# A decoder layer on one core: first cross-attention operands loaded in the interleaved pass, distance rows in the first phase

## What is computed

```python
x = x + attention(layernorm(x))                     # self-attention, 224 keys
x = x + cross_attention(layernorm(x), ctx)          # 750 keys, with a distance bias
x = x + mixture(layernorm(x))                       # 8 experts, the best 2 of each token
# cross-attention:
rel = abs(arange(Nk)[None, :] - arange(Nq)[:, None] - (Nk - Nq))
scores = einsum('bhqd,bhkd->bhqk', q, k) / sqrt(32) - slopes[:, None, None] * rel
attn = softmax(scores)
```

## Time and profile before

| | |
|---|---|
| median of 3 runs | 1952.62 us (1949.11 to 1953.68) |
| the profiled execution | 1952.63 us, span 1951.0 us |
| mean granted TensorE clock | 0.956 |
| TensorE / weight loads | 1771.3 us (91%) / 1423.1 us (73%) |
| VectorE | 1089.2 us (56%) |
| ScalarE | 761.1 us (39%) |
| GpSimd | 563.7 us (29%) |
| DMA | mean 160 GB/s |

### The profile page before, as it was taken

The page is one execution under the profiler, slowest core; times in us unless marked ns, Lnnn a source line. Parts: engine busy times, 40 slices in busy tenths (PEclk is TensorE's granted clock), DMA queues, the critical chain, the costliest instruction groups (busy, mean ns, idle before and its releaser), DMA issues. The chain is left out here.

```text
span 1951.0 us, 35771 instructions
## 1 busy us (share of the span) xinstructions
PE 1771.3 (91%) x11824; PEld 1423.1 (73%) x11824; DVE 1089.2 (56%) x1865; ACT 761.1 (39%) x1376; POOL 563.7 (29%) x597
## 2 busy tenths in 40 slices
PE   6997999999998866999999999649999999999997
PEld 5886777777777754777777777438787787887776
DVE  5543555555555524767777677374554545446553
ACT  3223334444434323655455554232442424224432
POOL 0001111111111102444454454251433425215541
PEclk9997999999999986999999999759999999999999
DMA  7636665565656349967576671153674637355753
GB/s 236 201 137 167 179 172 156 157 195 158 190 174 172 97 117 175 178 148 158 124 161 146 145 156 47 49 186 122 210 237 113 210 108 225 104 172 185 265 167 86
DMA packets 210770, 311.41 MB, mean 160 GB/s; under 512 B 20520, under 2 KB 149992, under 8 KB 206008
## 3 DMA queue, kind: packets, MB, share of 16 engines
q1 hardware_dynamic: 186208, 222.24, 42.9%
q0 software_dynamic: 14288, 41.26, 9.5%
q10 hardware_dynamic: 10160, 46.38, 6.5%
HBM read 226.07 MB, written 83.74 MB: 159 GB/s over the span
## 5 line engine op out<-in xcount | busy, mean ns | idle before, releaser
L1725 DVE TENSOR_REDUCE a_part_max<-a_s_bank 112x1 f32<-112x500 f32 (+1 forms) x384 | 238.0, 673 | 108.4 <-PE a_s_bank L1500 77.8
L1640 ACT ACTIVATE a_prob<-a_st_bank 125x448 f32<-125x448 f32 x384 | 195.0, 545 | 125.3 <-PE a_st_bank L1518 88.3
L2321 DVE TENSOR_TENSOR e_u_sb<-e_u_bank,e_b_row 128x512 f32<-128x512 f32 x138 | 95.0, 689 | 244.5 <-PE e_u_bank L2076 244.5
L2074 PE MATMUL e_u_bank<-e_w_hi,e_xT_hi 128*128 128x512 f32 x552 | 221.6, 401 | 2.6 <-DVE e_xT_lo L2309 1.9
L2076 PE MATMUL e_u_bank<-e_w_hi,e_xT_lo 128*128 128x512 f32 x552 | 217.4, 394 | 0.0
L2075 PE MATMUL e_u_bank<-e_w_lo,e_xT_hi 128*128 128x512 f32 x552 | 216.4, 392 | 0.0
L1423 POOL TENSOR_TENSOR a_part_sum<-a_prob 125x448 f32<-125x448 f32 x128 | 146.6, 1145 | 184.0 <-ACT a_prob L1640 184.0
L1500 PE MATMUL a_s_bank<-a_k_st,a_q_st 104*112 104x500 f32 (+1 forms) x512 | 159.9, 356 | 37.4 <-DMA a_k_st<-k 23.3
L2144 ACT ACTIVATE e_g_hi<-e_g_bank 128x256 fp32r<-128x256 f32 x137 | 52.6, 384 | 331.7 <-PE e_g_bank L2083 321.7
L1518 PEld LDWEIGHTS a_st_bank<-a_q_st,a_k_st 104*125 104x125 f32 x768 | 146.8, 198 | 45.1 <-ACT a_prob L1640 16.0
L1518 PE MATMUL a_st_bank<-a_q_st,a_k_st 104*125 104x224 f32 x768 | 155.9, 287 | 15.3 <-ACT a_prob L1640 13.3
(11 more groups left out here) (300 smaller groups left out, 4152.9 us busy)
## 6 DMA issues: line engine op xcount, KB each, us to landing
e_w_raw<-L_ffn_Wl SPq DMA_DIRECT2D x96, 512.0 KB, 10.0
a_k_st<-k SPq DMA_DIRECT2D x96, 375.0 KB, 6.0
e_b_row<-L_ffn_bl ACTq DMA_DIRECT2D x35, 1024.0 KB, 5.8
k<-m_kt_hi SPq DMA_DIRECT2D x48, 250.0 KB, 2.9
k<-m_kt_lo SPq DMA_DIRECT2D x48, 250.0 KB, 3.7
m_c_in<-ctx POOLq DMA_DIRECT2D x12, 896.0 KB
m_q_st<-q SPq DMA_DIRECT2D x96, 112.0 KB, 3.1
m_k_st<-k SPq DMA_DIRECT2D x96, 112.0 KB, 3.0
```

What stands on the lines that cost most here:

```text
L1640: act.activation(prob[:, s % 2, hh, 2 * u:2 * u + 2, :], st_bank[n % SB][0:CR, 0:2 * S].rearrange("p (e q) -> p e q", e=2), ACT.Exp).then_ ...
L1725: dve.tensor_reduce(out, scores, AX.X, ALU.max).then_inc(s_free, 1)
L2074: pe.matmul(out, xT_hi[:, slot, k, :], w_h, start=(k == 0), stop=False)
```

## The change

Three parts.

The operands of cross step 0, with their distance rows, get a tensor of their own, `first` (16 KB in a partition), which outlives the interleaved pass. It lies where the raw weights of the first phase lay; these get two slots in place of three, so that each weight is loaded behind the one it replaces. In step 28 of the interleaved pass SyncE loads `first` with eight DMAs (`load_first`).

The distance rows are made in the first phase. GpSimd makes the ramps and the key rows and stores the latter, all after it has issued the loads of chunks 1 and 2. The 16 query slopes are tied to the 16 query and key blocks of chunks 1 and 2 (`head_beside`): two operations on ScalarE, one on VectorE, a store from GpSimd's queue for each head; `q_rows` has one buffer.

In the cross-attention SyncE loads, for steps 1, 2 and 3 in turn, distance rows, queries and keys, and the values of the step before; then the router's biases and weights; then operands of step 4, values 3, `w_raw` and `out_bias`. `small_loaded` counts three transfers. x1 of the first sequence is loaded and gets its bias in steps 2 and 3, and the output weights are split in step 3 in place of 2.

```diff
-    raw_at = {"wq": 0, "wk": 1, "wv": 2, "wo": 0, "m_wk": 1, "m_wv": 2, "m_wq": 0}
+    raw_at = {"wq": 0, "wk": 1, "wv": 0, "wo": 1, "m_wk": 0, "m_wv": 1, "m_wq": 0}
...
+        grid = c.sb("z_grid", [R8, S])
+        is_lo = c.sb("z_is_lo", [R8, 1])
+        k_lin = c.sb("z_k_lin", [R8, CTX])
+        q_lin = c.sb("z_q_lin", [R8, S])
+        q_lin_hi = c.sb("z_q_lin_hi", [R8, S], F32R)
+        q_rows = c.sb("z_q_rows", [R8, S], F32R)
...
+        def head_beside(n, ch, m):
+
+            at = ring_of(n, ch, m) - 2 * KT
+            return at if 0 <= at < HEADS else None
...
                 load_w("wk")
-                load_w("wv")
                 sp.dma_start(v_bias[:, :], biases["wv"].partition_broadcast(P)).then_inc(bias_loaded, DMA)
-                load_w_behind("wo", "wq")
+                load_w_behind("wv", "wq")
                 for ch in range(CHUNKS):
                     for m in range(KT):
                         store_t("wq", ch, m)
                     if ch == 0:
-                        load_w_behind("m_wk", "wk")
+                        load_w_behind("wo", "wk")
                     if ch == 1:
-                        load_w_behind("m_wq", "wo")
+                        load_w_behind("m_wv", "wo")
                     for m in range(KT):
                         store_t("wk", ch, m)
                     if ch == 0:
-                        load_w_behind("m_wv", "wv")
+                        load_w_behind("m_wk", "wv")
+                    if ch == 1:
+                        sp.wait_ge(w_ready["m_wk"], KT)
+                        sp.sem_inc(turn, 1)
+                        load_w("m_wq")
...
+                load_x(1)
+                load_x(2)
...
+                for hh in range(4):
+                    for fill in (1.0, 0.0):
+                        then(pool.affine_select(out=k_lin[0:4, :], in_=k_lin[0:4, :], compare_op=ALU.not_equal, fill=fill, base=-hh,
+                                                pattern=[[0, CTX]], channel_multiplier=1))
+                        if fill:
+                            pool.dma_start(k_rows_out[:, hh, :], k_lin[:, :]).then_inc(krows_stored, DMA)
+                            pool.wait_ge(krows_stored, (hh + 1) * DMA)
+                load_x(3)
...
+                for hd in range(HEADS):
+                    pool.wait_ge(qrows_ready, hd + 1)
+                    pool.sem_inc(turn, 1)
+                    pool.dma_start(q_rows_out[:, hd // 4, hd % 4, :], as_f32(q_rows[:, :])).then_inc(qrows_stored, DMA)
+                pool.wait_ge(qrows_stored, HEADS * DMA)
...
+                    if head_beside(n, ch, m) is not None:
+                        query_slopes(head_beside(n, ch, m))
+
+                def query_slopes(hd):
+                    act.wait_ge(grid_ready, 1)
+                    if hd:
+                        act.wait_ge(qrows_ready, hd)
+                    act.activation(q_lin[:, :], grid[:, :], ACT.Copy, scale=slope(hd))
+                    act.activation(q_lin_hi[:, :], grid[:, :], ACT.Copy, scale=slope(hd)).then_inc(qlin_ready, 1)
...
+                    hd = head_beside(n, ch, m)
+                    if hd is not None:
+                        dve.wait_ge(qlin_ready, hd + 1)
+                        if hd:
+                            dve.wait_ge(qrows_stored, hd * DMA)
+                        dve.scalar_tensor_tensor(q_rows[:, :], as_f32(q_lin_hi[:, :]), is_lo[:, :], q_lin[:, :], ALU.mult, ALU.add).then_inc(qrows_ready, 1)
...
+def first_parts(first):
+
+    rows = 3 * DH + 8
+    return (first[0:rows, 0:4 * S].rearrange("p (h t) -> p h t", h=4),
+            first[0:rows, 4 * S:4 * (S + CTX)].rearrange("p (h t) -> p h t", h=4))
...
+                def load_first():
+
+                    first_q, first_k = first_parts(first)
+                    for i in range(RING):
+                        sp.wait_ge(k_stored[i], RING * 2 * DMA)
+                    for m in range(KT):
+                        sp.wait_ge(q_stored[m], 2 * DMA)
                     sp.sem_inc(turn, 1)
...
+                    for r, (q_part, k_part) in enumerate(zip(QUERY_PARTS, KEY_PARTS)):
+                        rows = slice(DH * r, DH * r + DH)
+                        for tile, dram, part, n in ((first_q, q2, q_part, S), (first_k, k2, k_part, CTX)):
+                            sp.dma_start(as_f32(tile[rows, :, :]), dram[0, part, :, 0:n].rearrange("(h p) t -> p h t", p=DH)).then_inc(first_loaded, DMA)
+                    sp.dma_start(as_f32(first_k[KA:KA + 8, :, :]), k_rows).then_inc(first_loaded, DMA)
+                    sp.dma_start(as_f32(first_q[KA:KA + 8, :, :]), q_rows[:, 0, :, :]).then_inc(first_loaded, DMA)
...
-                    if s in (7, 8, 9, 10):
-                        store_key_rows(s - 7)
-                    if s in (12, 14, 16, 18):
-                        store_query_rows((s - 12) // 2)
+                    if s == STEPS - 4:
+                        load_first()
...
+        first_q, first_k = first_parts(first)
+        q_st = [first_q] + [c.sb(f"a_q_st{i}", [KB, 4, S], F32R) for i in range(1, SLOTS)]
+        k_st = [first_k] + [c.sb(f"a_k_st{i}", [KB, 4, CTX], F32R) for i in range(1, SLOTS)]
...
-                load_qk(0)
-                load_qk(1)
-                load_v(0)
-                sp.dma_start(w_raw[:, :, :], w_out.rearrange("(k p) n -> p k n", p=P)).then_inc(w_loaded, DMA)
-                sp.dma_start(out_bias[:, :], b_out.partition_broadcast(P)).then_inc(small_loaded, DMA)
+                def load_rows(i):
+                    sp.dma_start(as_f32(k_st[i][KQ:KB, :, :]), k_rows).then_inc(rows_loaded[i], DMA)
+                    sp.dma_start(as_f32(q_st[i][KQ:KB, :, :]), q_rows[:, i, :, :]).then_inc(rows_loaded[i], DMA)
+
+                for i in range(1, SLOTS):
+                    load_rows(i)
+                    load_qk(i)
+                    load_v(i - 1)
                 sp.dma_start(r_bias[:, :], b_route.partition_broadcast(QR)).then_inc(small_loaded, DMA)
                 sp.dma_start(c_bias[:, :], choice_bias.partition_broadcast(QR)).then_inc(small_loaded, DMA)
                 sp.dma_start(wr_raw[:, :], w_route).then_inc(small_loaded, DMA)
-                load_qk(2)
-                load_v(1)
-                load_qk(3)
-                load_v(2)
-                load_v(3)
+                load_qk(SLOTS)
+                load_v(SLOTS - 1)
+                sp.dma_start(w_raw[:, :, :], w_out.rearrange("(k p) n -> p k n", p=P)).then_inc(w_loaded, DMA)
+                sp.dma_start(out_bias[:, :], b_out.partition_broadcast(P)).then_inc(bias_loaded, DMA)
                 for s in range(STEPS):
-                    if s + SLOTS < STEPS:
+                    if s + SLOTS < STEPS and s:
                         load_qk(s + SLOTS)
-                        if s:
-                            load_v(s + SLOTS - 1)
+                        load_v(s + SLOTS - 1)
                     elif s + SLOTS == STEPS:
                         load_v(STEPS - 1)
...
                 pool.sem_inc(rel_ready, 1)
-                load_x(0)
                 then(pool.memset(ones[:, :], 1.0))
                 then(pool.iota(iota_e[:, :, :], pattern=[[0, 4], [1, EXPERTS]], base=0, channel_multiplier=0, allow_small_or_imprecise_dtypes=True))
                 then(pool.memset(before[:, 0, :], 0.0))
                 pool.sem_inc(const_ready, 1)
-                pool.wait_ge(small_loaded, 4 * DMA)
-                add_out_bias(0)
...
+                    if s == 2:
+                        load_x(0)
+                    if s == 3:
+                        pool.wait_ge(bias_loaded, DMA)
+                        add_out_bias(0)
...
-                diagonal_rests(0)
                 for hh in range(4):
                     maxima(0, hh)
-                    if hh == 1:
-                        diagonal_rests(1)
+                    if hh < 2:
+                        diagonal_rests(hh)
                 row_maxima(0)
                 diagonal_rests(2)
-                dve.wait_ge(small_loaded, 4 * DMA)
+                dve.wait_ge(small_loaded, 3 * DMA)
                 for s in range(-1, STEPS):
-                    if s == 2:
+                    if s == 3:
```

183 lines of the change are left out of this document (66 added, 117 removed).

## The result

The changed kernel takes 1962.04 us (median of 5 runs, 1960.35 to 1962.75), the kernel before, run beside it, 1953.13 us (5 runs): ratio 1.0044, interval 1.0029 to 1.0059. It is slower by about 8.6 us, clear of the interval. The forecast was 1958.3. The profiled execution of the changed kernel took 1962.16 us, its span is 1960.5 us against 1951.0.

A forecast was written before the change was run, and what follows sets the result against it. TensorE, busy 91% of the span, was taken as the bound, so only its waits could earn. The sum was 1952.6 + 3.7 (seam) + 2 (first phase) + 0 = 1958.3 us, range 1945 to 1971.

The forecast's parts named there:

- +3.7 us was the term: Seam into the cross-attention: VectorE's restart after the small loads at 763.0 against 759.3; bounds -2.0 and +9.
- with the same surplus 6.7 MB must move: Seam: 6.01 MB stand ahead of the small loads, plus the 0.7 MB that overtook in the kernel before.
- the two rates that the prediction weighed: Seam: DMA at 182 GB/s, or 162 GB/s for queries, keys and values alone; restart at 761.3 or 765.9.
- The term was +2: First phase: query-row loops cost TensorE 1 us at the end of each of chunks 1 and 2; bounds 0 and +34.
- the prediction's own signs of being wrong: Step 1's maxima before 755, VectorE's q_rows waits over 10 us in the first phase, or TensorE's DMA wait near 660.
- The loop itself: First phase, VectorE: combine 0.43, store landing 2.3 and 0.2 make 2.9 us per row, 0.5 over the block time.
- the other edits have one answer: [...] 0: First phase: weights loaded behind those they replace, and key rows made on GpSimd in chunk 0, each cost 0.
- the cover that it names: First phase: TensorE's four spare product banks cover 4 x 2.43 = 9.7 us of VectorE's lag.
- The rows' removal from the pass: Interleaved pass: ScalarE's 32 and VectorE's 4 distance-row operations go, which caused TensorE no idle time; worth 0.
- The early landing: Rival at the seam: small loads overtake or VectorE isn't held; -21 with +2 gives 1934; chance 0.10.
- The store loop's rival: First phase: VectorE waits for each head's store; a 3.7 us landing adds 5 us a chunk, 1966; chance 0.14.
- same: Total time within about 0.3%, 5.9 us, which can't be told from no change; chance 0.43.

The follow-up runs named there:

- e4: Changed kernel with GpSimd's two loads of context rows (1 MB) issued behind the sixteen row stores: 1967.94 us, 1.0066 of the kernel before.
- e2: Changed kernel with the four value stores of chunk 1 issued ahead of the query weights' load: 1959.39 us, 1.0039 of the kernel before.
- e9: Changed kernel with VectorE's small-loads wait at step 3, chunk 1's value stores ahead of the query weights, two query-row buffers: 1934.19 us, 0.9915 of before.
- e3: Changed kernel with query distance rows made for head 0 only, its row stored sixteen times without waits between: 1952.7 us, 0.9998 of before.
- e8: Changed kernel with small-loads wait at step 3, value stores ahead of query weights, query rows made in interleaved steps 7 to 22: 1928.92 us, 0.9869.
- e1: Changed kernel with VectorE's wait for the small loads moved from ahead of its loop to step 3: 1940.02 us, 0.9938 of the kernel before.
- e7: Kernel before with VectorE's wait for the small loads moved from ahead of its loop to step 2: 1954.74 us, 1.0002 of the kernel before.
- e5: Changed kernel with two buffers for the query distance rows, VectorE waiting for the store before the last: 1957.86 us, 1.0028 of before.

## Why the prediction was right or wrong

The seam. Right: TensorE starts with the phase; step 0's maxima are 10.7 us behind the first load (11 foreseen); VectorE and TensorE then stand with `a_wr_raw` as releaser, 26.0 us (29 foreseen). So the mechanism, a second wait that swallows the first one's gain, held. Wrong in size: +3.7 us was the term, -0.2 the measure. The step that was mis-sized is "with the same surplus 6.7 MB must move". In the kernel before more moved than stood ahead: 0.7 MB to 757, and at 181 GB/s over the 37.6 us to the restart 1.2 MB, with the loads of step 2 issued right behind the small ones from 745.4 on. In the changed kernel nothing stands behind them: SyncE's next load is issued at 776.66. So 6.01 MB had to move, not 6.7, and from the first load to VectorE's restart 37.3 us went by: 6.01 MB in 37.3 us is 161 GB/s, and 161 GB/s is what the trace has from 731 to 768.5 (168 to 766). Of the two rates that the prediction weighed, 162 was right; the quantity wasn't.

The first phase. The term was +2, the measure +7.6, and here the forecast lost most of its distance. One of the prediction's own signs of being wrong came: VectorE's waits for `q_rows` are 15.8 us, over the 10 it named. The loop itself was right: 2.9 foreseen, 2.8 measured, of which 1.8 us from issue to VectorE's restart (72.87 to 74.63; 2.3 taken). Two steps failed. One is that the landing was priced by kind and not by what stands ahead of it on its queue: the first store waited behind 1.5 MB, which the diff shows just above the loop; e4 prices that at 3.4 us. The other is "the other edits have one answer: [...] 0". The weights' new order puts a wait and 1 MB ahead of the value stores of chunk 1. e2 prices that at 3.5 us, and e9 shows that with both mended chunk 1 is back to 35.7 us. What is left stands in chunk 2, 2.1 us, of which e9 leaves 0.5: the loop of the later rows and the clock, which no run tells apart. Here a slip of the prediction shows no effect: it lets VectorE fall behind in four key blocks of a chunk, but by the code all eight blocks carry a row, 4 us and not 2, still inside the cover that it names. The clock stands at 0.50 from 98.5 to 105, behind TensorE's wait, and costs only from 102.2 on, in chunk 2; in e9 and e3 it isn't there.

The rest. The load in step 28 cost 0, as foreseen: TensorE has no wait for a DMA from 640 to 700, though the DMA engines are busier there (share 0.67 from 643 to 668). The rows' removal from the pass gave nothing that its scatter shows, as foreseen, and e8 puts them back at no cost that its pass (557.0 us, inside 552.0 to 558.0) shows. `w_raw`, `out_bias` and x1 later: 0 (1182.3 against 1182.2 us to the end). The +2.0 us of the pass weren't foreseen and needn't be: the pass of the kernel before varies as much.

The rivals. The early landing, 1934, didn't come, but e1 shows that its price was right: 21 us with the wait gone, 21 foreseen. The store loop's rival said 1966 for a landing over 3.0 us; the landing was 1.8, and its loss came nevertheless, by the first store and the value stores. The sum: 1952.6 + 7.6 + 2.0 - 0.2 + 0.1 = 1962.1.

So the total came near partly by luck. The seam was put 3.9 us too high and the first phase 5.6 too low, and the two errors cancel but for 1.7 us; the other 2.0 of the 3.8 us by which the forecast was off is the scatter of the pass. And of the three outcomes "same" had the largest chance, 0.43, by a hair over "slower", 0.42, which came.

## What to carry to other kernels

When a change takes away the wait that ends first, read the next instruction of every engine behind it: here one count of three small loads, placed where it cost nothing, ate 21 us as soon as the first wait was gone, and moving it by three steps turned a loss of 0.4% into a gain of 0.6%. A store whose buffer is needed soon should not stand behind a megabyte on its own queue (4.3 and 4.9 us of waits here), nor beside one on another (5.3 us in e4). And a date counted from the start of the span carries the scatter of all that lies ahead: by such dates two mended waits seemed to hide each other, by the lengths of the chunk they add.

## What was not expected of the hardware

- One 128x128 subtraction on VectorE took 3.66 us in place of 0.28 beside five GpSimd operations that followed each other without a pause (e7). They came together because GpSimd had been held by the same small loads.
- A store of 7 KB from GpSimd's queue: 1.8 us from issue to the waiting engine's restart with the queue empty, 6.8 us (65.00 to 71.83) behind 1.5 MB.
- TensorE's idle time can be paid twice. Its wait at the end of chunk 1 is 6.6 us in the changed kernel, and its clock is then 0.50 to 105; in e5 it is 4.6 us, with a clock of 0.59 from 101.5 to 105; in e2 3.1 us, with 0.52 there; in e3 2.5 us, and the clock stays at 1.00. The rows of e5 and then e3, columns as in the earlier trace rows:

```profile
101.50:105.00 3.50, 3.50 (x12) 3.11 (x12) 0.00 (x0) 0.00 (x0) 0.00 (x0) 0.59 0.18 56
```
```profile
101.50:105.00 3.50, 3.50 (x19) 3.25 (x18) 1.37 (x2) 0.63 (x1) 0.00 (x0) 1.00 0.36 131
```
